# Row maxima for the attention's softmax from the high parts alone, each head of a pair on its own row strip of TensorE

## The reference

```
kqv = h @ Wqkv + bqkv                      # heads of 32 features
scores = einsum('bsnh,btnh->bnst', k, q) / sqrt(32)
scores = triu(scores) + -10000.0 * tril(ones_like(scores), k=-1)
attn = softmax(scores, axis=2)
out = einsum('bnkq,bknh->bqnh', attn, v).reshape(b, s, 512) @ Wo + bo
```

## Time and profile before

| | |
|---|---|
| runs, us | 2158.68, 2159.29, 2154.5 (median 2158.68) |
| the profiled execution | span of 2154.8 us from first to last instruction; the page tells no time around it |
| TensorE, VectorE, ScalarE, GpSimd busy | 87%, 58%, 39%, 31% |
| mean granted clock of TensorE | 0.937 |
| line 645, maxima's matmuls | 768, 216.3 us busy |

### The profile page before, as it was taken

One profiled execution on the slowest core, in us unless ns is written; L12 is line 12 of the kernel. 1 busy time (PEld: TensorE's weight loads), 2 busy tenths in 40 slices (PEclk: granted clock), 3 DMA queues, 4 the chain that ended last, 5 costly groups with the idle time before them and its releaser, 6 DMA issues. The chain is left out here.

```text
span 2154.8 us, 34842 instructions
## 1 busy us (share of the span) xinstructions
PE 1876.2 (87%) x9947; PEld 1191.8 (55%) x9948; DVE 1248.7 (58%) x3033; ACT 846.6 (39%) x1408; POOL 677.2 (31%) x762
## 2 busy tenths in 40 slices
PE   4799988999989899898999985799999959999990
PEld 0555543655544655444645532577777747888870
DVE  3456657356667356566356653755555556675567
ACT  1325555245554145463255560322222204555441
POOL 0101115101116001125011124655445569650066
PEclk8789999989999899999899997899999979999995
DMA  5312231321231222222222305222222267754498
GB/s 206 89 28 47 60 104 40 90 53 45 51 89 63 66 60 60 60 59 69 59 59 60 79 1 196 84 93 92 88 88 93 93 226 249 249 169 148 139 333 325
DMA packets 107081, 229.60 MB, mean 107 GB/s; under 512 B 23704, under 2 KB 23704, under 8 KB 106924
## 3 DMA queue, kind: packets, MB, share of 16 engines
q1 hardware_dynamic: 81968, 166.89, 25.9%
q0 software_dynamic: 14848, 50.34, 6.8%
q10 hardware_dynamic: 10112, 10.51, 1.6%
HBM read 111.23 MB, written 66.12 MB: 82 GB/s over the span
## 5 line engine op out<-in xcount | busy, mean ns | idle before, releaser
L401 ACT ACTIVATE pr<-sc 128x1024 f32<-128x1024 f32 (+3 forms) x384 | 307.9, 811 | 265.0 <-PE sc L670 245.0
L325 POOL TENSOR_SCALAR_AFFINE_SELECT pr<-pr 128x256 f32<-128x256 f32 x256 | 105.7, 413 | 952.1 <-ACT pr L401 951.9
L690 PE MATMUL O<-pr,V 128*32 128x512 f32 (+3 forms) x3072 | 328.3, 501 | 14.5 <-ACT oD L413 14.4
L514 DVE TENSOR_REDUCE mx<-ring 128x1 f32<-128x512 f32 x256 | 169.5, 678 | 240.4 <-PE ring L645 238.9
L510 DVE CUSTOM_DVE_ANT_0 ring<-ring,mask 128x512 f32<-128x512 f32 (+3 forms) x512 | 240.8, 511 | 67.0 <-PE ring L645 64.7
L670 PE MATMUL sc<-stk 128*128 128x512 f32 (+3 forms) x768 | 245.0, 401 | 15.0 <-ACT pr L401 12.9
L670 PEld LDWEIGHTS sc<-stk 128*128 128x128 f32 x768 | 116.9, 191 | 255.2 <-ACT pr L401 155.0
L645 PE MATMUL ring<-stk 96*128 96x512 f32 (+3 forms) x768 | 216.3, 381 | 10.2 <-DVE mx L510 4.7
L645 PEld LDWEIGHTS ring<-stk 96*128 96x128 f32 x768 | 144.2, 202 | 57.3 <-DVE mx L510 18.9
L636 PE MATMUL ring<-hhi,whi 128*128 128x512 f32 x256 | 112.0, 437 | 27.8 <-DVE hlo L489 15.8
L539 DVE RECIPROCAL oD<-oD 128x128 f32<-128x128 f32 x128 | 117.6, 934 | 28.4 <-ACT oD L413 28.4
(11 more groups left out here) (277 smaller groups left out, 3806.4 us busy)
## 6 DMA issues: line engine op xcount, KB each, us to landing
stk<-st SPq DMA_DIRECT2D x384, 128.0 KB, 2.4
x_e<-xs SPq DMA_DIRECT2D x79, 256.0 KB, 2.6
ys<-y_e SPq DMA_DIRECT2D x79, 256.0 KB, 2.1
xt<-in_L_attn_x_dram ACTq DMA_DIRECT2D x16, 512.0 KB, 6.2
st<-in_L_attn_x_dram SPq DMA_DIRECT2D x32, 256.0 KB, 2.7
x1d<-pr SPq DMA_DIRECT2D x32, 256.0 KB, 2.0
raw_e<-in_L_ffn_w_up_dram POOLq DMA_DIRECT2D x16, 512.0 KB, 5.1
raw_e<-in_L_ffn_w_down_dram POOLq DMA_DIRECT2D x16, 512.0 KB, 5.9
```

Of the source, the lines that this page charges most:

```text
L325: nc.gpsimd.affine_select(out=t, in_=t, compare_op=ALU.is_ge, fill=0.0, base=0, pattern=[[0, 2], [1, P]], channel_multiplier=-1).then_inc( ...
L401: nc.scalar.activation(pr[:, g % PRB, :, off:], sc[g % 2][:, :, off:], ACT.Exp, scale=SCALE).then_inc(exp_done, 1)
L514: nc.vector.tensor_reduce(mx[:, heads[0]:heads[-1] + 1, qt, part], bank[:, 0:len(heads) * w].rearrange("p (e k) -> p e k", e=len(heads)), ...
L690: last = nc.tensor.matmul(O[row:row + 32, off:], V[:, col:col + DH], pr[:, g % PRB, e, off:], start=(i == 0), stop=(i == 4 * c + 3))
```

## The change

The maximum is taken of high part times high part alone, which is 32 rows instead of 96. Head 0 of a pair uses rows 0 to 31 of the stack, head 1 rows 32 to 63; for that, head 1's first operand is stacked low, high, high instead of high, low, high, and its second as before (high, high, low), so that rows 32 to 63 hold the two high parts and the full product is the same sum in another order. The two matmuls of a unit are issued one behind the other, each into its own bank; both banks are waited for ahead of the first. Each head always has a bank of its own, and two narrow pieces (256 and 128 columns) share it: ten units, 20 banks, 24 matmuls. `M_DUE` counts units: 2, 3, 4 up to 10, so four banks in step 0 and two in each step to step 8. `m_reduce` runs once per bank, over one or two pieces, with the no-op ahead of all.

```diff
-    MUSES = []
-    for qt in reversed(range(NT)):
...
-            if 2 * n <= CH:
-                MUSES.append(((0, 1), qt, k0, n, part))
-            else:
-                MUSES += [((e,), qt, k0, n, part) for e in range(2)]
-    NM = len(MUSES)
-    M_DUE = [min(NM, -(-NM * (s + 1) // M_STEPS)) for s in range(NST)]
+    MUSES = [((qt, k0, min((qt + 1) * P - k0, CH), k0 // CH),) for qt in reversed(range(NT)) for k0 in (0, CH) if k0 < (qt + 1) * P]
+    joined = [i for i, (piece,) in enumerate(MUSES) if piece[2] <= CH // 2]
+    for i, j in reversed(list(zip(joined[0::2], joined[1::2]))):
+        MUSES[i] += MUSES.pop(j)
+    NMU = len(MUSES)
+    NM = 2 * NMU
+    M_DUE = [min(NMU, -(-NMU * (s + 1) // M_STEPS)) for s in range(NST)]
...
-            ring += ["m"] * (M_DUE[s] - (M_DUE[s - 1] if s else 0))
+            ring += ["m"] * (2 * (M_DUE[s] - (M_DUE[s - 1] if s else 0)))
...
-                            for n, part in enumerate(parts):
+                            for n, part in enumerate((((0, 1, 0), (1, 0, 0))[e], (2, 2, 3))[which]):
...
             def m_reduce(b, p, n):
-                heads, qt, k0, w, part = MUSES[n]
+                unit, e, at = MUSES[n // 2], n % 2, 0
                 bank = rb[ring_at("m", NM * p + n) % 3]
                 dve.wait_ge(m_done, b * NPAIR * NM + p * NM + n + 1)
-                if k0 <= qt * P < k0 + w:
-                    apart(dve)
...
+                apart(dve)
+                for qt, k0, w, part in unit:
+                    o = bank[:, at:at + w]
+                    at += w
+                    if k0 <= qt * P < k0 + w:
                         last = nc.vector.tensor_tensor_reduce(out=o, in0=o, in1=K.mask[:, CH - w:CH], scale=1.0, scalar=MASKED,
                                                               op0=ALU.add, op1=ALU.max, accum_out=mx[:, e, qt, part:part + 1])
-                    last.then_inc(m_red, 1)
...
+                    else:
+                        last = nc.vector.tensor_reduce(mx[:, e:e + 1, qt, part], o, AX.X, ALU.max)
+                last.then_inc(m_red, 1)
...
-                        while n < M_DUE[s]:
+                        while n < 2 * M_DUE[s]:
                             m_reduce(b, p + 1, n)
...
             def m_scores(b, p, n):
-                heads, qt, k0, w, part = MUSES[n]
-                bank = bank_for(b, "m", NM * p + n)
-                for x_, e in enumerate(heads):
-                    last = nc.tensor.matmul(bank[:, x_ * w:(x_ + 1) * w], K.stk[0:96, p % NSLOT, 0, e, qt * P:(qt + 1) * P],
-                                            K.stk[0:96, p % NSLOT, 1, e, k0:k0 + w], start=True, stop=True)
-                last.then_inc(m_done, 1)
+                banks = [bank_for(b, "m", NM * p + 2 * n + e) for e in range(2)]
+                at = 0
+                for x_, (qt, k0, w, part) in enumerate(MUSES[n]):
+                    for e in range(2):
+                        rows = slice(DH * e, DH * e + DH)
+                        last = nc.tensor.matmul(banks[e][:, at:at + w], K.stk[rows, p % NSLOT, 0, e, qt * P:(qt + 1) * P],
+                                                K.stk[rows, p % NSLOT, 1, e, k0:k0 + w], start=True, stop=True)
+                        if x_ == len(MUSES[n]) - 1:
+                            last.then_inc(m_done, 1)
+                    at += w
...
-                for n in range(NM):
+                for n in range(NMU):
                     m_scores(b, 0, n)
```

More of the change, by code:

```diff
@@ L174, in attention_phase @@
     ND = len(DIAG)
-    MUSES = []
-    for qt in reversed(range(NT)):
[L178 to L182, removed]
-            if 2 * n <= CH:
-                MUSES.append(((0, 1), qt, k0, n, part))
-            else:
-                MUSES += [((e,), qt, k0, n, part) for e in range(2)]
-    NM = len(MUSES)
-    M_DUE = [min(NM, -(-NM * (s + 1) // M_STEPS)) for s in range(NST)]
+    MUSES = [((qt, k0, min((qt + 1) * P - k0, CH), k0 // CH),) for qt in reversed(range(NT)) for k0 in (0, CH) if k0 < (qt + 1) * P]
[5 more added lines that the diff above has]
+    M_DUE = [min(NMU, -(-NMU * (s + 1) // M_STEPS)) for s in range(NST)]
+    assert all(sum(w for _, _, w, _ in unit) <= CH for unit in MUSES)
     MT_AT = M_STEPS + 1
@@ L282, in _ @@
                         apart(sp)
-                    for which, parts in enumerate(((0, 1, 0), (2, 2, 3))):
+                    for which in range(2):
                         sp.wait_ge(p_lo, b * 16 + 4 * (p // 2) + 2 * which + 2)
@@ L502, in m_reduce @@
             def m_reduce(b, p, n):
-                heads, qt, k0, w, part = MUSES[n]
+                unit, e, at = MUSES[n // 2], n % 2, 0
                 bank = rb[ring_at("m", NM * p + n) % 3]
                 dve.wait_ge(m_done, b * NPAIR * NM + p * NM + n + 1)
-                if k0 <= qt * P < k0 + w:
-                    apart(dve)
-                    for x_, e in enumerate(heads):
-                        o = bank[:, x_ * w:(x_ + 1) * w]
+                apart(dve)
[3 more added lines that the diff above has]
+                    if k0 <= qt * P < k0 + w:
                         last = nc.vector.tensor_tensor_reduce(out=o, in0=o, in1=K.mask[:, CH - w:CH], scale=1.0, scalar=MASKED,
                                                               op0=ALU.add, op1=ALU.max, accum_out=mx[:, e, qt, part:part + 1])
-                    last.then_inc(m_red, 1)
[L513 to L516, removed]
+                    else:
+                        last = nc.vector.tensor_reduce(mx[:, e:e + 1, qt, part], o, AX.X, ALU.max)
+                last.then_inc(m_red, 1)
             def m_rows(b, p):
```

## The result

The changed kernel takes 2211.1 us, the median of four runs (2206.9 to 2219.0), against 2158.1 in four runs of the kernel before: 1.0248 times the time, with a 95% interval of 1.0223 to 1.0273. The forecast was 2191 with a range to 2225. The profiled execution spans 2207.2 us where the one before spanned 2154.8, so 52.4 us are to be found.

What follows compares the result with a forecast made beforehand. TensorE was taken to bound the pair loop, VectorE the first phase. Odd pairs 7.9, pairs 5 -0.7, even pairs 7.6, pairs 6 2.8 and first phases 15.2 sum to +33 us: 2191 us on the median, range 2163 to 2225.

Steps and rivals of the forecast that it cites:

- the likeliest case: Whole kernel: strips side by side, switches eating the gain, wait paid; 2191 us, own range 2174 to 2206, chance 0.68.
- the strips in turn: Rival, maxima in the pair loop: a unit's two matmuls run one after another; 2222 us, chance 0.13.
- Side by side: Maxima of a pair's two heads: two row strips run together, a 512-wide unit costing 0.23 us instead of 0.47.
- The switch of shape: Nine of a pair's twelve steps: changing to 32 rows costs 0.21 us, 0.10 of draining and 0.11 of uncovered load.
- The free switch: Rival, pair loop: 32 rows follow 128 without draining and with weights loaded ahead; 2148 us, chance 0.08.
- The wait for two banks: Step 0 of a pair: the second unit waits for a reduction, weighted sums come 1.12 us later, +2.48 against +1.36.
- the third rival: Pair loop: step 0's wait for two banks and its like are hidden; 2166 us, chance 0.11.
- The first phase: First pair's maxima ahead of the loop: VectorE idles between units, +3.8 us per batch, 15.2 for four.
- Odd pairs: Pairs without projections in the loop: 1.12 - 0.35 + 0.11 = +0.88 us each, 7.9 for nine.
- Pairs 2 and 4: Even pairs, with projections: waits and switches less what step 4 saves, +0.63 us each, 5.0 for eight.
- Pairs 0: First pair of each batch in the loop: taken like the other even pairs, +0.63 us each, 2.5 for four.
- Pairs 5: Pair 5 in batches 0 to 2: ScalarE's loads cover step 0's wait, -0.24 us each, -0.7 for three.

Runs made afterwards that it cites:

- b: The changed kernel with both heads' maxima on rows 0 to 31, so a unit's two matmuls can't run together: 2294.0 us, 1.0649 times the kernel before.
- a: The changed kernel with TensorE waiting for one bank at a time, the 32-row strips kept: 2210.4 us, 1.0234 times the kernel before.
- f: The changed kernel with one bank at a time and 96 rows, its banks, order and no-op kept: 2157.9 us, 1.0000 times the kernel before.
- c: The changed kernel with 96 rows for the maxima again, the wait for two banks kept: 2188.5 us, 1.0137 times the kernel before.
- h: Kernel a with one full 128-row, 512-column matmul added in each of nine steps of pair 6: 2196.4 us, 1.0182 times the kernel before.
- e: The changed kernel with both heads' maxima on rows 0 to 63, one matmul after the other: 2253.3 us, 1.0446 times the kernel before.
- d: The changed kernel with the no-op ahead of masked banks only, as before the change: 2211.2 us, 1.0225 times the kernel before.

## Why the prediction was right, and where it was not

The direction held, and the mechanism of the likeliest case is what the runs show: strips side by side, switches that eat their gain, and a wait for two banks that is paid. The range held by luck. 2211 lies above the 2174 to 2206 that the prediction gave this case, and is inside the range only because that reached on to the strips in turn, which b excludes. Step by step:

- **Side by side:** right. 0.49 us for two wide matmuls against 0.73 in turn (b). The strips in turn, the first rival, fall with it. The row that the prediction drew on was weaker than it said: eight matmuls of 256 columns one after another would take about 0.9 us (half of 0.23 each), 1.6 times the 0.57 read there and not several times that.
- **The switch of shape:** right in size. From the scores' last matmul to the first maxima 0.32 us, and 0.49 to 0.50 for that one, as forecast from the earlier trace rows; with one bank at a time the gain in an odd pair is nil (a against f). The free switch falls. Steps 3 to 7 of an odd pair together gain 0.34 us, for 0.35 forecast; a slip in the sum (by its own terms a 384-column unit loses 0.04, not 0.01) didn't matter.
- **The wait for two banks:** right. The weighted sums of step 0 start 2.44 us behind the scores (forecast 2.48), with a wait of 0.85 on line 509 between the units. c shows the wait alone at +30 us, about the whole forecast, so the third rival, a wait that is hidden, falls too. VectorE starts 0.11 behind a matmul, not 0.15.
- **The first phase:** right, 3.6 to 3.9 per batch for 3.8 (the cycle of a plain unit adds up to 1.70, not 1.69).
- **Odd pairs:** +1.0 each for +0.88. What is missing is in step 10, 3.27 us instead of 2.92 where 0.11 was forecast: a small copy of VectorE's on the way to the transposes takes twice as long (below).
- **Pairs 2 and 4:** +0.51 at full clock for +0.63, but by misses that offset each other. In pair 2 step 0 adds 0.84 (forecast 0.89) and step 2 0.18 (0.19), step 4 saves 1.09 (0.70), step 6 adds 0.29 (0.16) and step 10 0.35 (0.11).
- **What failed: the clock inside the loop.** The prediction took TensorE's clock as low only ahead of the loop and left the pairs at 1.00 as in the earlier trace rows. Three terms were mis-sized by that. *Pairs 0* were forecast as other even pairs, +0.63, and measured +1.75 to +2.32: the half-clock stretch of the first phase, 17.0 us before in batch 1 (430.0 to 447.0), is 23.9 (441.6 to 465.5) and reaches 8.0 us into the pair instead of 4.5. *Pairs 5* were forecast at -0.24 and measured -0.02, +0.94 and +0.97: the half-clock stretch behind ScalarE's loads is as long as before (6.8 us), but in batches 1 and 2 it begins 1.8 to 1.9 us later in the pair and lies on 22 matmuls instead of 16 and 20; in batch 0 it lies on 16 as before. *One odd pair and one pair 4* fell to half clock in mid-loop, for 10.5 and 1.5 us more than their kind.

These terms make up the 20 us by which the change was slower than forecast: 10.5 + 1.5 + 5.3 (pairs 0) + 2.6 (pairs 5) = 19.9. The other terms are each off by 1.3 us or less, some up and some down, and cancel. That all of the 5.3 and the 2.6 is the clock is read from where the stretches lie; no run isolates it.

My first theory after the result, that the wait for two banks is the loss and the strips only fail to pay, holds in half. With the wait gone the time stays at 2210 (a). The strips' price is then switches and the clock: from pair 0's first scores to the end of pair 6 batch 1 takes a 217.3 us and f 205.4. Of the difference pair 6 is 5.3, pair 4 2.6, pair 0 2.4, pair 2 1.1, pair 5 0.6, and pairs 1 and 3 together -0.1. Only pair 6 has a run, h, that shows the clock to be the cause.

The Trainium skill, "TensorE: Matmul & The Clock Gate", section "What's actually happening", has the clock follow how busy TensorE has lately been. By that, a's pair 6 should hold its clock as the kernel before does. The trace differs: in the matching stretch of pair 6 the kernel before is busy less, and its clock holds.

```profile
631.30:637.90 6.60, 5.21 (x30) 2.25 (x28) 6.60 (x14) 2.43 (x3) 2.17 (x4) 1.00 0.00 0
```

Over the last 3.3 us of these stretches, too, TensorE is busy for 2.43 us in a, 2.40 in f and 2.10 in the kernel before. Busy time as the profile counts it is thus not the whole of what counts, and a against f, and b against e, point at the rows in use.

**What stays open.** Why the change, with its extra waits, keeps its clock in pair 6 (25.74 us at 1.00) where a loses it in every batch, and loses it instead once in an odd pair and once in a pair 4, isn't settled; one execution of it was profiled. Nor is whether it is the rows as such or the weights and data that go through them, nor why the clock comes back after 6.8 us in one batch of e and after 30.7 in two. A filler in pair 4 and in the odd pairs wasn't tried. No version here beats the kernel before; f ties with it.

## What to carry to other kernels

Halving the columns that a line streams gains only what is left after each change of array shape (about 0.21 us here, 0.44 for a unit that cost 0.47), so it should pay more to put small-row matmuls next to each other than to alternate them with full ones, which wasn't tried here. A handshake that takes two of three buffers at once removes the one that hid the latency; price it in the step where two units stand in a row. And where a change takes work out of TensorE, look at the granted clock stretch by stretch in the trace after, and time it with enough runs: less work, or thinner work, can cost more in clock than it saves.

## What the runs showed of the hardware that was not expected

**The clock falls with thin matmuls at equal busy time.** 5.47 of 6.60 us busy with strips of 32 rows, then 13.7 us at half clock (a); 5.21 (before) or 5.62 (f) of 6.60 with 96 rows, and no fall, all in pair 6. Adding full matmuls there kept the clock and took 14 us off the median (h). That the rows are the reason is not isolated: b and e speak for it in how often the clock falls, not in how long it stays low.

**A small copy beside GpSimd takes twice as long.** Copies of 128 x 16 elements between SBUF tiles, by line, ns, minimum, median and maximum: before, then after.

```profile
L530 DVE COPY S<-mhi x32: 180/183/185, 126.7 to 1265.8; 128x16 f32<-128x16 f32 x32
```
```profile
L524 DVE COPY S<-mhi x32: 181/366/374, 131.8 to 1317.7; 128x16 f32<-128x16 f32 x32
```

In order of time in pair 1 of the kernel after, the copy lies within GpSimd's masking of the exponentials:

```profile
514.87 0.41 POOL L320 TENSOR_SCALAR_AFFINE_SELECT pr<-pr 128x256 f32<-128x256 f32 x1 [0.88 <-ACT pr L396]
514.94 0.37 DVE L524 COPY S<-mhi 128x16 f32<-128x16 f32 x1
```

Before, the chain of small operations came at another moment. In c the copy starts ahead of GpSimd's masking and takes 0.18 us, and the operation behind it, which starts 0.05 us into the masking in pair 1, takes 0.40:

```profile
L525 DVE TENSOR_TENSOR S<-negm,mhi x32: 171/394/400, 129.7 to 1295.6; 128x16 f32<-128x16 f32 x32
```

In the traces of before, after, a, c, d and f, 101 of these two small operations start within a masking (0.02 us or more behind its start and 0.15 or more ahead of its end) and take 0.27 to 0.40 us each; the other 283 take 0.17 to 0.19. So the delay goes with the overlap throughout, whichever of the two it hits. That the two engines get in each other's way is what this says; no run moved the one against the other by itself.
